# Layer 1 of a two-layer interaction kernel: the first two of its four groups go from whole fp32 matmuls to three high and low passes

## The chip, the cores and the metric

The kernel runs on one core of one Trainium2 chip. The metric is the time of one execution on the device in microseconds, the median of several runs. Engines are named as in the profile: PE is TensorE, DVE is VectorE, ACT is ScalarE, POOL is GpSimd, SP is SyncE.

## The reference

512 samples have 32 embeddings each of 32 numbers, gathered from 32 tables. Two interaction layers follow; then the sums over the last axis, joined with 16 dense numbers, go through three small dense layers.

```python
e = stack([tbl_f[ids[:, f]] for f in range(32)], axis=1)      # 512 x 32 x 32
x0, prev = e, e
for W in (filter_0, filter_1):                                # 1024 x 128 and 4096 x 128
    z = einsum('bhd,bmd->bhmd', x0, prev)                     # all pairs of fields
    z = z.reshape(b, h * m, d)
    prev = relu(einsum('bpd,pn->bnd', z, W[0]))
    outs.append(prev)
z = sum(concatenate(outs, axis=1), axis=-1)                   # 512 x 256
h = relu(concatenate([z, dense_ctx]) @ W_top1 + b_top1)
h = relu(h @ W_top2 + b_top2)
y = h @ W_top3
```

All is float32.

## The kernel before, in words

The batch is cut into 32 chunks of 16 samples, 512 columns (sample and embedding position) each; a chunk has four tiles of 128 columns.

**Layer 1.** A chunk's input lies 128 partitions wide in `x_shift` (four groups of shifted fields) and `x_same`. DVE multiplies them in `products`: `which` 0 makes groups 0 and 1 of `z` (one instruction of 128x1024, L520), `which` 1 makes groups 2 and 3, and `which` 2 makes `z_last` (L524), the half shift that needs its own rows. PE adds the groups into one bank, `acc1`, in `layer1` (L742 and after). Groups 0 and 1 (`WHOLE` is 2) are one fp32 matmul each (L751; the profile records it as two). Groups 2 and 3 (`SPLIT` is 2), from chunk 3 on, are three matmuls each of the type fp32r (L756): high weights by high rows, low weights by high rows, high weights by low rows. The high rows, `z_hi`, are ACT's rounding copy of both groups (`round_pair`, L397); the low rows, `z_lo`, are DVE's subtraction z - z_hi, one 128x512 instruction for each group (`lower_pair`, L530). The last matmul (L760) takes `z_parts`, whose rounding is ACT's (`round_last`, L392) and whose low third is POOL's (`lower_last`, L274). ACT then makes two copies of relu(acc1) (`relu1`, L379 and L384), and DVE makes the low part of the first (`lower`, L539).

**Layer 2.** For each tile PE fills eight banks, three fp32r matmuls for each (L784 to L786). By the order `ADADADAD` four banks go to ACT (`t_act`, a ring of three) and four to DVE (`t_dve`, a ring of four). ACT multiplies each quarter of its banks by a weight per partition (`weigh_tile`, L420); DVE multiplies each quarter of its own and adds it to what ACT left in `prod` (`add_tile`, L573 and L577, 16 instructions a tile). The first of DVE's additions of a tile waits for ACT's first bank of that tile. POOL then folds `prod` to one block: a DMA that adds one half to the other (`halve`, L283), then two additions, 128x512 and 128x256 (L303), and a third into `side` (L309). `halve` of a tile waits for ACT and DVE to be done with that tile; POOL issues `halve` of tile i and right behind it folds tile i-1.

**Order.** No planner is used: each engine's program is written out. In a chunk c of the steady state:

- PE: layer 2 of tile 0; groups 0 and 1 of layer 1 of chunk c+1; layer 2 of tile 1; the rest of layer 1 of c+1; layer 2 of tiles 2 and 3.
- DVE: `transpose` (L506) of c+1; tile 0; `lower_pair` of c+1; tile 1; `products` 0 and 2 of c+2; tile 2; `lower` of c+1; `sum2` (L597, L600) of c-1; tile 3; `products` 1 of c+2; `pooling1` (L548) of c+1.
- ACT: tile 0; `round_pair` of c+1; tile 1; `relu1` of c+1; tile 2; `relu2` of c-1 (L404); `round_last` of c+2; tile 3.
- POOL: for each tile in turn, two gathers of chunk c+3 (L264, tiles 0 and 1 only), `halve` of this tile, the fold of the tile before; at the end of the chunk `lower_last` of c+2.
- SP: the transposing round trip of the embeddings through device memory and the loads of `x_same`, `x_shift` and `x_pair`.

Of the kernel before, what the change touches and what calls it, by code (L numbers as in the profile page):

```python
# [6 lines left out]
MAPS = 128  # L7
# [5 lines left out]
RUN = TILES * DIM  # L13
SHIFTS = 4
GROUPS = 4
SPLIT = 2
WHOLE = GROUPS - SPLIT
BANK = 512
X_REST = 3 + 1

# [21 lines left out]
LEAD = 3  # L42


def dlrm_tower(nc, table, ids, dense, w0a, w0b, w0c, w1, wt1, bt1, wt2, bt2, wt3, identity, spread, out):
# [5 lines left out]
    with ExitStack() as ctx:  # L51
# [3 lines left out]
        def sem(name):  # L55
            return ctx.enter_context(nc.semaphore(name))
# [9 lines left out]
        x_shift = [sb(f"x_shift{p}", [128, GROUPS, COLS]) for p in range(2)]  # L66
        x_pair = [sb(f"x_pair{p}", [3 * FIELDS, 2, COLS]) for p in range(2)]
        z = [sb(f"z{p}", [128, GROUPS, COLS]) for p in range(2)]
        z_hi = sb("z_hi", [128, SPLIT, COLS], f32r)
        z_lo = sb("z_lo", [128, SPLIT, COLS], f32r)  # L70
        z_last = [sb(f"z_last{p}", [3 * FIELDS, COLS]) for p in range(2)]
        z_parts = [sb(f"z_parts{p}", [3 * FIELDS, COLS], f32r) for p in range(2)]
        v = sb("v", [128, GROUPS, MAPS])
        v_hi = sb("v_hi", [128, SPLIT, MAPS], f32r)
        v_lo = sb("v_lo", [128, SPLIT, MAPS], f32r)
        v_last = sb("v_last", [3 * FIELDS, MAPS])
        v_parts = sb("v_parts", [3 * FIELDS, MAPS], f32r)
        cur1 = [sb(f"cur1_{p}", [128, COLS]) for p in range(2)]
# [12 lines left out]
        turned2 = sb("turned2", [128, TILES * MAPS])  # L91
        pool2 = sb("pool2", [128, MAPS // DIM, TILES, CHUNKS])
        pool1 = sb("pool1", [128, TILES, CHUNKS * QUARTERS])
        ctx_sb = sb("ctx_sb", [CTX, BATCH])
        wt1_ctx = sb("wt1_ctx", [CTX, TOP1])
        bt1_sb = sb("bt1_sb", [128, T1])
        bt2_sb = sb("bt2_sb", [128, T2])
        wt3_sb = sb("wt3_sb", [128, T2])
# [5 lines left out]
        wt2_raw = w_raw[:, 2 * TOP1:2 * TOP1 + T1 * TOP2].rearrange("p (k n) -> p k n", k=T1)  # L104
        spare = 2 * TOP1 + T1 * TOP2 + T2 * BATCH
        pick = w_raw[:, spare:spare + QUARTERS * PICK].rearrange("x (q n) -> x q n", q=QUARTERS)
        h2 = w_raw[:, 2 * TOP1 + T1 * TOP2:2 * TOP1 + T1 * TOP2 + T2 * BATCH].rearrange("n (f b) -> n f b", f=T2)

        pool1_hi, pool1_lo = (sb(f"pool1_{half}", [128, BATCH], f32r)[:, :] for half in ("hi", "lo"))
        h1 = z[0]  # L110

        h1_hi, h1_lo = (w[:, 0:T1 * BATCH].rearrange("n (f b) -> n f b", f=T1) for w in (w_hi, w_lo))
# [32 lines left out]
        weigh_ready = sem("weigh_ready")  # L145
        z_ready = sem("z_ready")
        z_rounded = sem("z_rounded")
        pair_rounded, z_lo_ready = sem("pair_rounded"), sem("z_lo_ready")

        z_parts_ready = sem("z_parts_ready")  # L150
# [49 lines left out]
        @block.sync  # L200
        def _(sp):
            sp.dma_start(raw_ids[:, :], ids).then_inc(ids_loaded, 16)
            sp.dma_start(spread_sb[:, :, :], spread).then_inc(spread_loaded, 16)

            def chunk(c, p):
                turn = before(c, p) + 1

                wait(sp, layer1_done, c - 1)

                sp.wait_ge(gathered[p], turn * (16 * TILES))  # L210
                rows = x_rows[p].rearrange("h (q c) -> q h c", q=QUARTERS)
                sp.dma_start(rows[:, 0:FIELDS], emb[p][:, :]).then_inc(rows_written[p], 16)
                sp.dma_start(rows[:, FIELDS:2 * FIELDS], emb[p][:, :]).then_inc(rows_written[p], 16)

                sp.wait_ge(rows_written[p], turn * (16 * 2))
                src = x_rows[p]
                first, stride = src.offset, COLS
                pair = bass.AP(src.tensor, first, [[stride, FIELDS], [FIELDS // 2 * stride, 2], [1, COLS]])
                if c == 0:

                    sp.dma_start(x_pair[p][0:FIELDS, :, :], pair).then_inc(pair_zero, 16)
                    return

                def shifted(first_group, groups):

                    return bass.AP(src.tensor, first + first_group * stride,
                                   [[stride, FIELDS], [GROUPS * stride, SHIFTS], [1, groups * COLS]])

                sp.dma_start(x_same[p][:, :],
                             bass.AP(src.tensor, first, [[stride, FIELDS], [0, SHIFTS], [1, COLS]])).then_inc(x_first[p], 16)  # L230
                sp.dma_start(x_shift[p][:, 0:WHOLE, :].rearrange("p g c -> p (g c)"),
                             shifted(0, WHOLE)).then_inc(x_first[p], 16)
                for copy in range(3):
                    sp.dma_start(x_pair[p][copy * FIELDS:(copy + 1) * FIELDS, :, :], pair).then_inc(x_rest[p], 16)
                sp.dma_start(x_shift[p][:, WHOLE:GROUPS, :].rearrange("p g c -> p (g c)"),
                             shifted(WHOLE, SPLIT)).then_inc(x_rest[p], 16)

            def top_loads():

                sp.wait_ge(wl_ready, W_PIECES)  # L240
                sp.dma_start(ctx_sb[:, :], dense).then_inc(top_loaded, 16)
                sp.dma_start(pick[:, :, :], identity).then_inc(top_loaded, 16)
                sp.dma_start(wt1_raw, wt1[0:256, :].rearrange("(k p) n -> p k n", p=128)).then_inc(top_loaded, 16)
                sp.dma_start(wt1_ctx[:, :], wt1[256:256 + CTX, :]).then_inc(top_loaded, 16)
                sp.dma_start(bt1_sb[:, :], bt1).then_inc(top_loaded, 16)
                sp.dma_start(wt2_raw, wt2.rearrange("(k p) n -> p k n", p=128)).then_inc(top_loaded, 16)
                sp.dma_start(bt2_sb[:, :], bt2).then_inc(top_loaded, 16)
                sp.dma_start(wt3_sb[:, :], wt3).then_inc(top_loaded, 16)

            over_chunks(chunk, 4, top_loads)  # L250

            sp.wait_ge(y_ready, 1)
            sp.dma_start(out, y_sb[:, :]).then_inc(out_written, 16)
            sp.wait_ge(out_written, 16)
# [101 lines left out]
        def _(act):  # L356
# [29 lines left out]
            def round_last(c, p):  # L386
# [4 lines left out]
                wait(act, layer1_done, c - 1)  # L391
                nc.scalar.activation(z_parts[p][:, :], z_last[p][:, :], ACT.Copy).then_inc(z_rounded, 1)  # L392

            def round_pair(c, p):
                act.wait_ge(z_ready, c * 3 + 3)
                act.wait_ge(layer1_done, c)
                nc.scalar.activation(z_hi[:, :, :], z[p][:, WHOLE:GROUPS, :], ACT.Copy).then_inc(pair_rounded, 1)  # L397

            def relu2(c, p):

# [35 lines left out]
            def chunk(c, p):  # L436
                for i in range(TILES):
                    weigh_tile(c, i, p)
                    if i == 0 and not ((c < 2 or c + 1 >= CHUNKS)):
                        round_pair(c + 1, 1 - p)  # L440
                    if i == 2 and c == CHUNKS - 1:
                        upper_top(len(top_pieces) - 1)
                    if i == 1 and c == 0:
                        round_last(1, 1)
                    if i == 0 and 0 <= c - (CHUNKS - TOP_PEEL) < len(top_pieces) - 1:
                        upper_top(c - (CHUNKS - TOP_PEEL))
                    if i == 2 and not (c == 0):
                        relu2(c - 1, 1 - p)
                    if i == (2 if c == 0 else 1) and not (c + 1 >= CHUNKS):
                        relu1(c + 1, 1 - p)  # L450
                    if i == 0 and c == 1:
                        round_last(2, 0)
                    if i == 2 and not ((c == 0 or c + 2 >= CHUNKS)):
                        round_last(c + 2, p)

            for k in range(W_EARLY):
# [37 lines left out]
        def _(dve):  # L494
# [13 lines left out]
            def products(c, p, which):  # L508
# [14 lines left out]
                else:  # L523
                    nc.vector.tensor_tensor(z_last[p][:, :], x_pair[p][:, 0, :], x_pair[p][:, 1, :],  # L524
                                            ALU.mult).then_inc(z_ready, 1)

            def lower_pair(c, p):
                dve.wait_ge(pair_rounded, c - 2)
                for k in range(SPLIT):
                    nc.vector.tensor_tensor(z_lo[:, k, :], z[p][:, WHOLE + k, :], z_hi[:, k, :].bitcast(fp32),  # L530
                                            ALU.subtract).then_inc(z_lo_ready, 1)

            def lower(c, p):
# [59 lines left out]
            def sum2(c, p):  # L593
# [12 lines left out]
            nc.vector.tensor_tensor(v[:, :, :], v[:, :, :], v_b[:, :, :], ALU.add).then_inc(v_ready, 1)  # L606

            dve.wait_ge(v_ready, 1)
            nc.vector.tensor_copy(v_hi[:, :, :], v[:, WHOLE:GROUPS, :]).then_inc(v_ready, 1)
            dve.wait_ge(v_ready, 2)  # L610
            nc.vector.tensor_tensor(v_lo[:, :, :], v[:, WHOLE:GROUPS, :], v_hi[:, :, :].bitcast(fp32),
                                    ALU.subtract).then_inc(v_ready, 1)

            nc.vector.tensor_copy(v_parts[:, :], v_last[:, :]).then_inc(v_ready, 1)
# [41 lines left out]
            def chunk(c, p):  # L656
# [60 lines left out]
        def _(pe):  # L717
# [21 lines left out]
            def layer1(c, p, groups):  # L739
# [2 lines left out]
                    pe.wait_ge(lo_ready, c)  # L742
                    pe.wait_ge(cur1_ready, c)
                for g in groups:
                    if g < WHOLE or g < GROUPS and c <= 2:

                        if g == 0:
                            pe.wait_ge(z_ready, c * 3 + 1)
                        elif g == WHOLE:
                            pe.wait_ge(z_ready, c * 3 + 3)  # L750
                        nc.tensor.matmul(acc1[:, :], v[:, g, :], z[p][:, g, :], start=g == 0, stop=False)  # L751
                    elif g < GROUPS:
                        k = g - WHOLE
                        pe.wait_ge(z_lo_ready, (c - 3) * SPLIT + k + 1)
                        for weights, rows in ((v_hi, z_hi), (v_lo, z_hi), (v_hi, z_lo)):
                            nc.tensor.matmul(acc1[:, :], weights[:, k, :], rows[:, k, :], start=False, stop=False)  # L756
                    else:

                        pe.wait_ge(z_parts_ready, c)
# [195 lines left out]
```

## Time and profile before

| what | value |
|---|---|
| time, median of 3 runs | 865.25 us (864.55 to 865.81) |
| profiled execution, its own time | 865.07 us |
| its span, first to last instruction | 863.3 us |
| PE, DVE, ACT, POOL busy | 854.4, 778.2, 680.4, 655.3 us |
| granted TensorE clock, mean | 0.992 |

Busy time is the time in which at least one instruction of the engine was recorded as running. An instruction is recorded from when the engine takes it up, so in a run of DVE or ACT instructions each begins some 0.08 us ahead of the end of the one before, and an instruction that stands still for something inside the engine looks like a long one, not like idle time.

### The profile page before, as it was taken

How to read it: one execution, taken by the hardware profiler on the slowest of the kernel's cores; microseconds unless marked ns; L12 is line 12 of the kernel's file. 1: busy time of each engine (PE TensorE's matmuls, PEld its weight loads, DVE VectorE, ACT ScalarE, POOL GpSimd, SP SyncE). 2: the span in 40 equal slices, each digit the busy share in tenths (PEclk: the TensorE clock that was granted, in tenths of full speed). 3: DMA queues.
4: the chain of work that ended last, by engine and by line, in shares of the span. 5: the costliest groups of instructions: out<-in, count | busy, mean ns of one | idle time of the engine just before them, and what ended most of it. 6: DMA issues, size and time to landing. Idle time of an engine off the chain costs nothing.

```text
span 863.3 us, 13937 instructions
## 1 busy us (share of the span) xinstructions
PE 854.4 (99%) x3583; PEld 672.2 (78%) x3583; DVE 778.2 (90%) x2392; ACT 680.4 (79%) x2231; POOL 655.3 (76%) x677
## 2 busy tenths in 40 slices
PE   8999999999999999999999999999999999999998
PEld 3777787777778777777877777787777778777866
DVE  4889999999999999999999999999999999999952
ACT  3778888888888888888888888888888888888832
POOL 5577788888887888778788877778878878866740
PEclk9999999999999999999999999999999999999988
DMA  5878866668677666777666687766668776664500
GB/s 168 200 201 197 199 133 139 158 161 185 163 170 151 135 157 162 182 165 181 146 131 153 162 182 167 178 151 131 150 158 185 168 178 137 139 145 93 99 6 0
DMA packets 54949, 130.86 MB, mean 152 GB/s; under 512 B 8020, under 2 KB 18996, under 8 KB 54869
## 3 DMA queue, kind: packets, MB, share of 16 engines
q0 software_dynamic: 22240, 68.17, 42.9%
q1 hardware_dynamic: 31090, 59.13, 22.4%
q10 hardware_dynamic: 1539, 2.67, 0.9%
q8 instruction: 28, 0.46, 0.2%
q14 instruction: 52, 0.43, 0.1%
HBM read 59.69 MB, written 4.20 MB: 74 GB/s over the span
## 4 chain that ended last, share of the span: by engine, by line
PE 96%; DMA 2%; DVE 1%; POOL 0%; ACT 0%; issue 0%; SPq 0%; ACTq 0%
PE t_act L784 13%; PE t_act L786 13%; PE t_act L785 13%; PE t_dve L784 13%; PE t_dve L786 13%; PE t_dve L785 13%; PE acc L751 7%; PE acc L756 5%; PE t_act L794 1%; PE acc L760 1%; DMA x_rows<-emb 1%; PE t_dve L805 1%; PE t_dve L841 1%; PE t_act L862 0%; PE t_dve L855 0%; DVE prod L577 0%
## 5 line engine op out<-in xcount | busy, mean ns | idle before, releaser
L420 ACT ACTIVATE prod<-t_act,weigh 128x128 f32<-128x128 f32 x2048 | 576.5, 373 | 101.5 <-PE t_act L786 96.6
L577 DVE SCALAR_TENSOR_TENSOR prod<-t_dve,weigh,prod 128x128 f32<-128x128 f32 x1792 | 481.5, 342 | 9.4 <-PE t_dve L786 7.4
L303 POOL TENSOR_TENSOR prod<-prod 128x512 f32<-128x512 f32 (+1 forms) x255 | 296.8, 1164 | 19.6 <-DMA prod<-prod 8.8
L784 PE MATMUL t_act<-w_hi,cur_hi 128*128 128x512 f32 x512 | 212.3, 415 | 0.0
L786 PE MATMUL t_act<-w_hi,cur_lo 128*128 128x512 f32 x512 | 199.7, 390 | 0.0
L785 PE MATMUL t_act<-w_lo,cur_hi 128*128 128x512 f32 x512 | 199.6, 390 | 0.0
L784 PE MATMUL t_dve<-w_hi,cur_hi 128*128 128x512 f32 x512 | 199.5, 390 | 0.0
L786 PE MATMUL t_dve<-w_hi,cur_lo 128*128 128x512 f32 x512 | 199.3, 389 | 0.0
L785 PE MATMUL t_dve<-w_lo,cur_hi 128*128 128x512 f32 x512 | 199.1, 389 | 0.0
L283 POOL DMA_DIRECT2D prod<-prod x126 | 118.9, 944 | 104.6 <-ACT prod L420 63.2
L264 POOL DMA_INDIRECT emb<-table_dram,all_ids x128 | 163.8, 1279 | 40.0 <-issue 30.0
L784 PEld LDWEIGHTS t_act<-w_hi,cur_hi 128*128 128x128 f32 x512 | 96.2, 188 | 26.6 <-issue 8.0
L785 PEld LDWEIGHTS t_act<-w_lo,cur_hi 128*128 128x128 f32 x512 | 96.3, 188 | 26.3 <-issue 7.4
L785 PEld LDWEIGHTS t_dve<-w_lo,cur_hi 128*128 128x128 f32 x512 | 96.1, 188 | 20.6
L786 PEld LDWEIGHTS t_act<-w_hi,cur_lo 128*128 128x128 f32 x512 | 96.1, 188 | 20.6
L784 PEld LDWEIGHTS t_dve<-w_hi,cur_hi 128*128 128x128 f32 x512 | 96.1, 188 | 20.4
L786 PEld LDWEIGHTS t_dve<-w_hi,cur_lo 128*128 128x128 f32 x512 | 96.1, 188 | 20.4
L573 DVE SCALAR_TENSOR_TENSOR prod<-t_dve,weigh,prod 128x128 f32<-128x128 f32 x256 | 76.5, 340 | 36.4 <-ACT prod L420 33.1
L520 DVE TENSOR_TENSOR z<-x_shift,x_same 128x1024 f32<-128x1024 f32 x62 | 75.8, 1222 | 0.0
L309 POOL TENSOR_TENSOR side<-prod 128x128 f32<-128x128 f32 x127 | 61.4, 484 | 10.0
L751 PE MATMUL acc<-z,v 128*128 128x512 f32 x132 | 61.9, 591 | 0.0
L379 ACT ACTIVATE cur_hi<-acc 128x512 fp32r<-128x512 f32 x32 | 19.2, 599 | 39.4 <-PE acc L760 35.7
(93 smaller groups left out, 572.9 us busy)
## 6 DMA issues: line engine op xcount, KB each, us to landing
prod<-prod POOLq DMA_DIRECT2D x126, 512.0 KB, 5.1
x_shift<-x_rows SPq DMA_DIRECT2D x62, 512.0 KB, 5.9
x_pair<-x_rows SPq DMA_DIRECT2D x94, 128.0 KB, 4.3
x_same<-x_rows SPq DMA_DIRECT2D x31, 256.0 KB, 3.3
x_rows<-emb SPq DMA_DIRECT2D x64, 64.0 KB
w_raw<-w_dram ACTq DMA_DIRECT2D x8, 256.0 KB, 4.1
emb<-table_dram,all_ids POOLq DMA_INDIRECT x128, 2.9
w_raw<-wt_dram SPq DMA_DIRECT2D x2, 512.0 KB, 9.9
```

The source lines that it names most:

```text
L264: nc.gpsimd.indirect_dma_start(emb[p][:, i * DIM:(i + 1) * DIM], None, table, bass.IndirectOffsetOnAxis(ap=all_ids[:, c * TILES + i:c * TI ...
L283: nc.gpsimd.dma_start(prod[i][:, dst, :].rearrange("x h n -> x (h n)"), prod[i][:, other, :].rearrange("x h n -> x (h n)"), accum_op=ALU.a ...
L303: nc.gpsimd.tensor_tensor(src[:, dst, :], src[:, dst, :], src[:, other, :], ALU.add).then_inc(folded, 1)
L309: nc.gpsimd.tensor_tensor(side[p][:, i, :], src[:, 0, :], src[:, 1, :], ALU.add).then_inc(side_ready, 1)
L420: last = nc.scalar.activation(prod[i][:, HEADS * a + j, :], t_act[n % ARING][:, j * MAPS:(j + 1) * MAPS], ACT.Copy, scale=weigh[p][:, i, h ...
L520: nc.vector.tensor_tensor(z[p][:, g, :], x_shift[p][:, g, :], x_same[p][:, None, :].to_broadcast([128, 2, COLS]), ALU.mult).then_inc(z_rea ...
L573: nc.vector.scalar_tensor_tensor(dst, src, w, dst, ALU.mult, ALU.add).then_inc(added, 1)
L577: nc.vector.scalar_tensor_tensor(dst, src, w, dst, ALU.mult, ALU.add).then_inc(added, 1)
L751: nc.tensor.matmul(acc1[:, :], v[:, g, :], z[p][:, g, :], start=g == 0, stop=False)
L784: nc.tensor.matmul(bank[:, :], cur_hi[p][:, cols], w_hi[:, w], start=True, stop=False)
L785: nc.tensor.matmul(bank[:, :], cur_hi[p][:, cols], w_lo[:, w], start=False, stop=False)
L786: nc.tensor.matmul(bank[:, :], cur_lo[p][:, cols], w_hi[:, w], start=False, stop=True).then_inc(done, 1)
```

## The change

`z_hi`, `z_lo`, `v_hi` and `v_lo` hold all four groups. From chunk 3 on groups 0 and 1 are also three fp32r matmuls each, in the order of before. ACT has a new `round_first`, a rounding copy of groups 0 and 1 of chunk c+2, ahead of tile 3 of chunk c, where `round_last` was; `round_last` moves behind tile 3. DVE has a new `lower_first`, two subtractions of 128x512 for groups 0 and 1 of chunk c+2, behind tile 3 of chunk c: after `products` 1 of c+2 and ahead of `pooling1` of c+1. Both run in chunks 1 to 29. A new semaphore, `layer1_half`, tells ACT that PE has read the first two groups of the chunk before. The operands of the dense input and two of the top stage's tiles move into memory that is free by then.

```diff
-SPLIT = 2
-WHOLE = GROUPS - SPLIT
+WHOLE = GROUPS // 2
...
+            def round_first(c, p):
+
+                act.wait_ge(z_ready, c * 3 + 1)
+                act.wait_ge(layer1_half, c - 1)
+                nc.scalar.activation(z_hi[:, 0:WHOLE, :], z[p][:, 0:WHOLE, :], ACT.Copy).then_inc(first_rounded, 1)
...
-                    if i == 2 and not ((c == 0 or c + 2 >= CHUNKS)):
+                    if i == 2 and 0 < c < CHUNKS - 2:
+                        round_first(c + 2, p)
+                    if i == 3 and 0 < c < CHUNKS - 2:
                         round_last(c + 2, p)
...
+            def lower_first(c, p):
+                dve.wait_ge(first_rounded, c - LEAD + 1)
+                for g in range(WHOLE):
+                    nc.vector.tensor_tensor(z_lo[:, g, :], z[p][:, g, :], z_hi[:, g, :].bitcast(fp32),
+                                            ALU.subtract).then_inc(first_lo_ready, 1)
...
-            nc.vector.tensor_copy(v_hi[:, :, :], v[:, WHOLE:GROUPS, :]).then_inc(v_ready, 1)
+            nc.vector.tensor_copy(v_hi[:, :, :], v[:, :, :]).then_inc(v_ready, 1)
             dve.wait_ge(v_ready, 2)
-            nc.vector.tensor_tensor(v_lo[:, :, :], v[:, WHOLE:GROUPS, :], v_hi[:, :, :].bitcast(fp32),
+            nc.vector.tensor_tensor(v_lo[:, :, :], v[:, :, :], v_hi[:, :, :].bitcast(fp32),
...
                 if more2:
                     products(c + 2, p, 1)
+                    if c > 0:
+                        lower_first(c + 2, p)
                 if more1:
                     pooling1(c + 1, 1 - p)
...
-                    if g < WHOLE or g < GROUPS and c <= 2:
+                    if g < GROUPS and c < LEAD:
...
-                        pe.wait_ge(z_lo_ready, (c - 3) * SPLIT + k + 1)
-                        for weights, rows in ((v_hi, z_hi), (v_lo, z_hi), (v_hi, z_lo)):
-                            nc.tensor.matmul(acc1[:, :], weights[:, k, :], rows[:, k, :], start=False, stop=False)
+                        if g < WHOLE:
+                            pe.wait_ge(first_lo_ready, (c - LEAD) * WHOLE + g + 1)
+                        else:
+                            pe.wait_ge(z_lo_ready, (c - LEAD) * WHOLE + g - WHOLE + 1)
+                        nc.tensor.matmul(acc1[:, :], v_hi[:, g, :], z_hi[:, g, :], start=g == 0, stop=False)
+                        nc.tensor.matmul(acc1[:, :], v_lo[:, g, :], z_hi[:, g, :], start=False, stop=False)
+                        last = nc.tensor.matmul(acc1[:, :], v_hi[:, g, :], z_lo[:, g, :], start=False, stop=False)
+                        if g == WHOLE - 1:
+                            last.then_inc(layer1_half, 1)
```

## Rows read from the trace of the kernel before

**Rows 1.** Part 1 of the page: busy us, share of the span, instructions.
```profile
PE 854.4 (99%) x3583; PEld 672.2 (78%) x3583; DVE 778.2 (90%) x2392; ACT 680.4 (79%) x2231; POOL 655.3 (76%) x677
```

**Rows 2.** Part 4 of the page: the chain that ended last, by engine.
```profile
PE 96%; DMA 2%; DVE 1%; POOL 0%; ACT 0%; issue 0%; SPq 0%; ACTq 0%
```

**Rows 3.** Busy time by stretch: PE, PEld, DVE, ACT, POOL, clock, DMA, GB/s.
```profile
400.00:450.00 50.00, 50.00 (x215) 39.95 (x214) 47.17 (x149) 41.38 (x138) 40.75 (x43) 1.00 0.70 160
```

**Rows 4.** Who waited for whom: us in total, times, longest.
```profile
POOL prod L283 <- ACT prod L420: 63.2, 28, 2.7
...
DVE z_last L630 <- DMA x_pair<-x_rows: 3.5, 1, 3.5
```

**Rows 5.** The chain in order of time, 406 to 435: start us, us, what.
```profile
407.31 1.72 PE acc L751 x4
...
414.51 1.36 PE acc L756 x6
```

**Rows 6.** Groups by form: line, operation, count, busy us and mean ns, idle before.
```profile
L397 ACT ACTIVATE z_hi<-z 128x1024 fp32r<-128x1024 f32 x29 | 31.1, 1073 | 0.0
```

**Rows 7.** DVE's timeline over one chunk: start us, us, line, what.
```profile
405.53 0.57 DVE L573 SCALAR_TENSOR_TENSOR prod<-t_dve,weigh,prod 128x128 f32<-128x128 f32 x2
...
409.63 1.29 DVE L530 TENSOR_TENSOR z_lo<-z,z_hi 128x512 fp32r<-128x512 f32 x2
411.06 0.61 DVE L573 SCALAR_TENSOR_TENSOR prod<-t_dve,weigh,prod 128x128 f32<-128x128 f32 x2
...
415.59 1.22 DVE L520 TENSOR_TENSOR z<-x_shift,x_same 128x1024 f32<-128x1024 f32 x1
416.73 0.68 DVE L524 TENSOR_TENSOR z_last<-x_pair 96x512 f32<-96x512 f32 x1
418.36 0.61 DVE L573 SCALAR_TENSOR_TENSOR prod<-t_dve,weigh,prod 128x128 f32<-128x128 f32 x2 [0.95 <-ACT prod L420]
...
422.65 0.68 DVE L539 TENSOR_TENSOR cur_lo<-cur,cur_hi 128x512 fp32r<-128x512 f32 x1
...
428.72 1.22 DVE L520 TENSOR_TENSOR z<-x_shift,x_same 128x1024 f32<-128x1024 f32 x1
...
430.68 0.57 DVE L573 SCALAR_TENSOR_TENSOR prod<-t_dve,weigh,prod 128x128 f32<-128x128 f32 x2
```

**Rows 8.** POOL's timeline behind tile 3 of that chunk.
```profile
429.36 0.86 POOL L283 DMA_DIRECT2D prod<-prod  x1 [2.48 <-ACT prod L420]
429.95 2.42 POOL L303 TENSOR_TENSOR prod<-prod 128x512 f32<-128x512 f32 x2
```

**Rows 9.** DVE's timeline, a product and its follower near 768.
```profile
767.55 1.28 DVE L520 TENSOR_TENSOR z<-x_shift,x_same 128x1024 f32<-128x1024 f32 x1
768.75 2.18 DVE L524 TENSOR_TENSOR z_last<-x_pair 96x512 f32<-96x512 f32 x1
```

**Rows 10.** POOL's timeline at the same place.
```profile
768.18 0.87 POOL L283 DMA_DIRECT2D prod<-prod  x1 [0.43 <-issue]
768.78 2.76 POOL L303 TENSOR_TENSOR prod<-prod 128x512 f32<-128x512 f32 x2
```

**Rows 11.** DVE's timeline near 787: a pair of low parts.
```profile
787.12 3.38 DVE L530 TENSOR_TENSOR z_lo<-z,z_hi 128x512 fp32r<-128x512 f32 x2
```

**Rows 12.** POOL's timeline at the same place.
```profile
787.75 0.86 POOL L283 DMA_DIRECT2D prod<-prod  x1
788.35 2.75 POOL L303 TENSOR_TENSOR prod<-prod 128x512 f32<-128x512 f32 x2
```

**Rows 13.** DVE's timeline near 642.
```profile
643.05 0.95 DVE L524 TENSOR_TENSOR z_last<-x_pair 96x512 f32<-96x512 f32 x1
```

**Rows 14.** POOL's timeline at the same place.
```profile
642.12 1.33 POOL L309 TENSOR_TENSOR side<-prod 128x128 f32<-128x128 f32 x1
```

**Rows 15.** DVE's timeline near 52, chunk 1.
```profile
52.80 0.68 DVE L524 TENSOR_TENSOR z_last<-x_pair 96x512 f32<-96x512 f32 x1
```

**Rows 16.** POOL's timeline at the same place.
```profile
52.30 3.15 POOL L303 TENSOR_TENSOR prod<-prod 128x512 f32<-128x512 f32 x2
```

More of the change, by code:

```diff
@@ L68, in dlrm_tower @@
         z = [sb(f"z{p}", [128, GROUPS, COLS]) for p in range(2)]
-        z_hi = sb("z_hi", [128, SPLIT, COLS], f32r)
-        z_lo = sb("z_lo", [128, SPLIT, COLS], f32r)
+        z_hi = sb("z_hi", [128, GROUPS, COLS], f32r)
+        z_lo = sb("z_lo", [128, GROUPS, COLS], f32r)
         z_last = [sb(f"z_last{p}", [3 * FIELDS, COLS]) for p in range(2)]
@@ L73, in dlrm_tower @@
         v = sb("v", [128, GROUPS, MAPS])
-        v_hi = sb("v_hi", [128, SPLIT, MAPS], f32r)
-        v_lo = sb("v_lo", [128, SPLIT, MAPS], f32r)
+        v_hi = sb("v_hi", [128, GROUPS, MAPS], f32r)
+        v_lo = sb("v_lo", [128, GROUPS, MAPS], f32r)
         v_last = sb("v_last", [3 * FIELDS, MAPS])
@@ L106, in dlrm_tower @@
         pick = w_raw[:, spare:spare + QUARTERS * PICK].rearrange("x (q n) -> x q n", q=QUARTERS)
+        room = 2 * TOP1 + T1 * TOP2
+        ctx_sb = w_raw[0:CTX, room:room + BATCH]
+        wt1_ctx = w_raw[0:CTX, room + BATCH:room + BATCH + TOP1]
         h2 = w_raw[:, 2 * TOP1 + T1 * TOP2:2 * TOP1 + T1 * TOP2 + T2 * BATCH].rearrange("n (f b) -> n f b", f=T2)
-        pool1_hi, pool1_lo = (sb(f"pool1_{half}", [128, BATCH], f32r)[:, :] for half in ("hi", "lo"))
+        pool1_hi, pool1_lo = z_hi[:, 0, :], z_lo[:, 0, :]
         h1 = z[0]
@@ L147, in dlrm_tower @@
         z_rounded = sem("z_rounded")
+        layer1_half, first_rounded, first_lo_ready = sem("layer1_half"), sem("first_rounded"), sem("first_lo_ready")
         pair_rounded, z_lo_ready = sem("pair_rounded"), sem("z_lo_ready")
@@ L235, in chunk @@
                 sp.dma_start(x_shift[p][:, WHOLE:GROUPS, :].rearrange("p g c -> p (g c)"),
[L236 removed]
+                             shifted(WHOLE, GROUPS - WHOLE)).then_inc(x_rest[p], 16)
             def top_loads():
@@ L396, in round_pair @@
                 act.wait_ge(layer1_done, c)
-                nc.scalar.activation(z_hi[:, :, :], z[p][:, WHOLE:GROUPS, :], ACT.Copy).then_inc(pair_rounded, 1)
+                nc.scalar.activation(z_hi[:, WHOLE:GROUPS, :], z[p][:, WHOLE:GROUPS, :], ACT.Copy).then_inc(pair_rounded, 1)
             def relu2(c, p):
@@ L525, in products @@
                                             ALU.mult).then_inc(z_ready, 1)
+            def lower_first(c, p):
[3 more added lines that the diff above has]
+                                            ALU.subtract).then_inc(first_lo_ready, 1)
             def lower_pair(c, p):
                 dve.wait_ge(pair_rounded, c - 2)
-                for k in range(SPLIT):
-                    nc.vector.tensor_tensor(z_lo[:, k, :], z[p][:, WHOLE + k, :], z_hi[:, k, :].bitcast(fp32),
+                for g in range(WHOLE, GROUPS):
+                    nc.vector.tensor_tensor(z_lo[:, g, :], z[p][:, g, :], z_hi[:, g, :].bitcast(fp32),
                                             ALU.subtract).then_inc(z_lo_ready, 1)
@@ L750, in layer1 @@
                             pe.wait_ge(z_ready, c * 3 + 3)
-                        nc.tensor.matmul(acc1[:, :], v[:, g, :], z[p][:, g, :], start=g == 0, stop=False)
+                        last = nc.tensor.matmul(acc1[:, :], v[:, g, :], z[p][:, g, :], start=g == 0, stop=False)
+                        if g == WHOLE - 1:
+                            last.then_inc(layer1_half, 1)
                     elif g < GROUPS:
-                        k = g - WHOLE
-                        pe.wait_ge(z_lo_ready, (c - 3) * SPLIT + k + 1)
-                        for weights, rows in ((v_hi, z_hi), (v_lo, z_hi), (v_hi, z_lo)):
-                            nc.tensor.matmul(acc1[:, :], weights[:, k, :], rows[:, k, :], start=False, stop=False)
+                        if g < WHOLE:
[5 more added lines that the diff above has]
+                        last = nc.tensor.matmul(acc1[:, :], v_hi[:, g, :], z_lo[:, g, :], start=False, stop=False)
+                        if g == WHOLE - 1:
+                            last.then_inc(layer1_half, 1)
                     else:
```

2 lines of the change are left out of this document (removed).

## The prediction, made before the result was known

> **What bounds the kernel now.** I read the page's busy times first, then the chain, the busy time by stretch, the waits and last DVE's and POOL's timelines of one chunk. PE is busy 99% of the span [rows 1] and makes 96% of the chain [rows 2]; in a stretch of 50 us in the middle it is busy all 50, at the full clock, and DVE is busy 47.17 of the same 50 [rows 3]. So PE sets the period, and DVE stands close behind. From one tile 0 to the next is 430.68 - 405.53 = 25.15 us [rows 7]; I use 25.14, since PE repeats at that.
>
> What DVE would need if it never waited is less than its busy time, because an instruction that follows another starts inside the other's last 0.08 us. From starts in rows 7: tile 0 takes 409.63 - 405.53 = 4.10; the two low parts 1.29 - 0.08 = 1.21; tile 1 stands at 415.59 - 411.06 = 4.53, but is the same 16 instructions as tile 0, so 4.10 is work; products 0 and 2 take 1.14 + 0.60 = 1.74; tile 2 stands at 422.65 - 418.36 = 4.29, again 4.10 of work; from there through tile 3 428.72 - 422.65 = 6.07; the last product, the pooling and the transpose 430.68 - 428.72 = 1.96. The sum is 23.28 us of a 25.14 us period: 1.86 us to spare.
>
> **The change, part by part.** *PE.* Two fp32 matmuls (four records) take 1.72 us, the six fp32r matmuls that do the same for groups 2 and 3 take 1.36 [rows 5]. The first two groups change from the one to the other in chunks 3 to 31, 29 times: 29 x 0.36 = 10.4 us less. PE's own period becomes 24.78 us, and were PE to stay the bound, the profiled execution's 865.07 would become 854.7.
>
> *ACT.* One more rounding copy of 128x1024, 1.07 us [rows 6]. ACT is busy 41.38 of 50 us [rows 3], 20.8 of a period; with 21.9 of 24.78 it stays under PE. The copy goes ahead of tile 3, where a shorter one (the last part's rounding) leaves, so ACT's first bank of tile 3 is some 0.4 us late; DVE starts tile 3 only after 6.0 us of own work and, with what follows, later than before, which hides it. Uncovered it would be at most 0.4 us a chunk; I take 0. The last part's rounding, now behind tile 3, is read by POOL after its fold and by PE a chunk later; POOL stands idle 2.48 us ahead of that fold [rows 8], so 0.
>
> *DVE without disturbance.* Two more subtractions, 1.21 us by the pair that is there [rows 7]. The need becomes 23.28 + 1.21 = 24.49 us, 0.29 under PE's new period. DVE enters tile 0 some 1.2 us later against PE, but four banks are in its ring, and a bank takes it 4.10 / 4 = 1.03 us, so PE isn't held. Its wait for the rounding is met long before. If this were all, the answer would be 854.7.
>
> *DVE against POOL.* The place of the pair is what I take to decide. The trace holds five DVE instructions of two operands in ordinary memory that met POOL's folds. Near 768 a product ends at 767.55 + 1.28 = 768.83, the next starts at 768.75 and takes 2.18 us instead of 0.68 [rows 7, 9]; POOL's fold had started at 768.78, behind a `halve` from 768.18 to 769.05 [rows 10]. Near 788 the same: two low parts take 3.38 us instead of 1.29 [rows 11], the `halve` stands at 787.75 and the fold at 788.35 [rows 12]. Near 642 POOL's L309 takes 1.33 us, held until the product ahead is over, then runs first and the next DVE instruction takes 0.95 us, ending 644.00 - 643.45 = 0.55 us behind it [rows 13, 14]. So one of the two waits for the other to finish, and POOL, once there, got in between two DVE instructions that stood back to back. Against it: at 52.80 the product's follower ran undisturbed in 0.68 us while a fold that had started at 52.30 stood [rows 15, 16].
>
> Now the new place. Tile 3's end triggers `halve`; it starts 429.36 - 428.72 = 0.64 us behind the product's start and the fold 1.23 us behind it, for 2.48 us of idleness ahead show that POOL is ready and waits for exactly this event [rows 4, 8]. The product ends at 1.22. Today what follows is the pooling, which reads one operand, and it isn't held. In the changed kernel the first subtraction starts at 1.13. Against the product's end the `halve` then stands at -0.58 and the fold at +0.01; at 768 they stood at -0.65 and -0.05 and DVE lost. Since tile 3's end triggers both, this repeats in every chunk, however late DVE is.
>
> The price, with the product's start as 0: the subtraction ends as at 768, 770.93 - 768.78 = 2.15 us behind the fold's start, at 1.23 + 2.15 = 3.38, instead of 1.81. The fold's second step has queued up meanwhile; at 768 the two steps ended at 771.54, 0.61 us behind DVE's instruction. If that step gets in ahead of the second subtraction, as L309 did at 642, the latter ends at 3.38 + 0.61 + 0.55 = 4.54, instead of 1.13 + 1.29 = 2.42. So 2.12 us more a chunk; the bounds are 0 (52.80) and 2.2 (both held for whole folds, 1.6 + 0.6). I take 2.12, since 768 is the nearest row. DVE's need becomes 24.49 + 2.12 = 26.61, and DVE is the bound: 1.83 us over PE's period.
>
> The second low pair, behind tile 0, comes while POOL gathers [rows 7]; in the new order POOL's next `halve` is triggered by tile 0's end, and its fold would start near the end of that pair: POOL waits, not DVE. `lower` behind tile 2 may meet L309's end: 0 to 0.3 us, taken as 0, kept in the range.
>
> *The Trainium skill on this.* "SBUF — State Buffer", section "SBUF: two separate sides", says that DVE and GpSimd share one pair of ports, that a DVE instruction with two such inputs and a GpSimd instruction exclude each other for their whole length, and that whoever starts first has it. By that rule the first subtraction, which starts ahead of the fold, isn't held, and only the second is; the sum would be the second rival's. The row at 768 says otherwise, and the measurement decides.
>
> *The rest.* The weights' two conversions double, 0.3 to 0.7 us on DVE at the start, ahead of idle time of 3.5 us in which DVE waits for a DMA [rows 4]: 0, at most +0.7. The moved buffers cost nothing that I can see: same instructions, same queues, 0.
>
> **The sum.** 865.07 - 10.4 + 29 x 1.83 = 907.7. DVE can fall behind before PE stands still, and it makes that up in the last two chunks, which have no products: between one bank (1.03) and four (4.1), I take 3. That gives 904.7, say 905 us. The profiled execution is 0.18 us under the median of the runs, which changes nothing.
>
> **The rivals.** *No collision that counts* (DVE keeps its pair together as at 52.80, and POOL waits): PE stays the bound, 24.49 against 24.78, and the time is 854.7, up to 859 if DVE needs 0.15 more a chunk than I add up. For it: the row at 52.80, and that most low parts take 1.29 for two. Against it: those meet gathers, not folds. It is the case of the other side.
>
> *Only one of the two is held.* If the first passes and the fold enters ahead of the second: the first ends at 1.81, the fold 1.60 - 0.13 later (770.38, which is 0.55 ahead of DVE's end at 768, less 768.78; L309 at 642 saves 0.13 by having waited), the second 0.55 behind that, at 3.83, 1.41 late: DVE's need is 25.90 and the time 854.7 + 29 x 1.12 - 3 = 884. If only the first is held: 3.38 + 0.61 = 3.99, 1.57 late, 854.7 + 29 x 1.28 - 3 = 889. For them: the rule above; whether POOL's second step wins rests on one meeting at 642.
>
> *DVE's lateness feeds back through ACT or POOL* (relu1 later, PE waits for a low part, which delays tile 2 on DVE): PE can then lose up to 0.5 us a chunk on top, 905 + 14 = 919. For it speaks that tile 2 waited 0.95 us for ACT [rows 7]; against it, that a DVE that is late finds ACT done.
>
> **How the numbers follow.** Both held, 0.52, own range 896 to 914 (29 x 0.3 us either way). One held, 0.20. No collision that counts, 0.20. Feedback, 0.05. Something between, near 865, 0.03. The range 880 to 914 leaves out the fast case and little else. What this kernel can tell from no change is 0.2%, 1.7 us: faster 0.20, within 0.02, slower 0.78.
>
> **What would show it.** In the changed kernel's trace: PE's six passes for groups 0 and 1 in 1.36 us; a chunk period of 26.6 us; the two new subtractions at 2.2 and 1.16 us in place of 0.68 each, each ending 0.55 us behind a POOL addition; POOL's second step at 1.08 us instead of 0.74; idle time of PE of 1.8 us a chunk, ended by DVE; DVE nearly without idle time. New subtractions of 0.68 us each and a period of 24.8 us would make the prediction wrong, and a wait of PE ended by ACT or POOL would put the loss elsewhere.

## The result, and the profile after

The changed kernel takes 872.78 us (median of 4, 872.23 to 875.11), before 865.53 (864.55 to 868.05, 4 runs): a ratio of 1.009, interval 1.0065 to 1.0116. A later run of both gave 874.39 and 865.76, 1.0102 (1.0073 to 1.0131). It is slower, as forecast, but by 7 to 9 us and not by 40. The profiled execution took 872.23 us, its span is 870.4.

The page of the changed kernel: part 1, then the chain by engine, which answer to [rows 1] and [rows 2].

```profile
PE 858.7 (99%) x3641; PEld 676.1 (78%) x3641; DVE 824.7 (95%) x2450; ACT 699.2 (80%) x2260; POOL 708.8 (81%) x677
...
PE 69%; DVE 23%; issue 4%; DMA 2%; ACT 1%; POOL 0%; SPq 0%; DVEq 0%; ACTq 0%
```

PE's share of the chain fell from 96% to 69%, and DVE has 23%. The busy time of 250 us in the middle (PE, PEld, DVE, ACT, POOL, clock, DMA, GB/s), before and then after:

```profile
400.00:650.00 250.00, 250.00 (x1066) 199.78 (x1065) 236.24 (x738) 206.89 (x686) 203.38 (x209) 1.00 0.71 160
```

```profile
400.00:650.00 250.00, 249.62 (x1070) 198.25 (x1069) 249.66 (x747) 210.39 (x685) 220.76 (x208) 1.00 0.72 160
```

DVE went from 236.24 us to 249.66: it hardly ever stops. PE's busy share still looks full, but a matmul that waits for a bank is recorded as a long one, so the share hides it: the weight loads take 198.25 us, where the same program of PE with nothing to hold DVE (e5 below) gets through 206.84 in these 250 us. PE's waits tell it better. The waits of the changed kernel (us, times, longest):

```profile
PEld t_dve L808 <- DVE prod L592: 22.2, 47, 1.3
```

The row says that a weight load of PE waited for DVE to empty a bank. No such row exists before. DVE's timeline over one chunk of the changed kernel (start us, us, line), which answers to [rows 7], and POOL's of the same stretch, which answers to [rows 8]:

```profile
408.45 1.22 DVE L529 TENSOR_TENSOR z<-x_shift,x_same 128x1024 f32<-128x1024 f32 x1
409.58 1.29 DVE L539 TENSOR_TENSOR z_lo<-z,z_hi 128x512 fp32r<-128x512 f32 x2
...
411.61 0.57 DVE L588 SCALAR_TENSOR_TENSOR prod<-t_dve,weigh,prod 128x128 f32<-128x128 f32 x2
...
421.05 1.22 DVE L529 TENSOR_TENSOR z<-x_shift,x_same 128x1024 f32<-128x1024 f32 x1
422.18 0.69 DVE L533 TENSOR_TENSOR z_last<-x_pair 96x512 f32<-96x512 f32 x1
422.78 0.60 DVE L588 SCALAR_TENSOR_TENSOR prod<-t_dve,weigh,prod 128x128 f32<-128x128 f32 x2
...
426.92 1.64 DVE L554 TENSOR_TENSOR cur_lo<-cur,cur_hi 128x512 fp32r<-128x512 f32 x1
```

```profile
409.08 0.87 POOL L284 DMA_DIRECT2D prod<-prod  x1 [1.20 <-DVE prod L592]
409.85 2.99 POOL L304 TENSOR_TENSOR prod<-prod 128x512 f32<-128x512 f32 x2
...
421.10 2.08 POOL L310 TENSOR_TENSOR side<-prod 128x128 f32<-128x128 f32 x1
...
425.64 1.02 POOL L284 DMA_DIRECT2D prod<-prod  x1
426.28 2.88 POOL L304 TENSOR_TENSOR prod<-prod 128x512 f32<-128x512 f32 x2
```

Three things are to be seen. The new pair (L539 at 409.58) takes 1.29 us: it isn't held, and POOL's fold pays, 2.99 us for two additions instead of 2.42. DVE has next to no idle time: tile 2 no longer waits 0.95 us for ACT. And the low part behind tile 2 (L554, L539 of before) takes 1.64 us instead of 0.68, because POOL's fold has been running since 426.28. This last one takes 1.5 us or more in 20 of the 32 chunks. The period is 25.5 us (L554 at 401.41 and at 426.92), DVE's own 24.49 and 0.96.

The two-operand forms of DVE in the chunks, with their means (the last number but one) in the changed kernel:

```profile
L529 DVE TENSOR_TENSOR z<-x_shift,x_same 128x1024 f32<-128x1024 f32 x62 | 77.0, 1242 | 0.0
L554 DVE TENSOR_TENSOR cur_lo<-cur,cur_hi 128x512 fp32r<-128x512 f32 x32 | 44.1, 1380 | 1.1 <-ACT cur L385 1.1
L539 DVE TENSOR_TENSOR z_lo<-z,z_hi 128x512 fp32r<-128x512 f32 x58 | 38.4, 703 | 0.0
L545 DVE TENSOR_TENSOR z_lo<-z,z_hi 128x512 fp32r<-128x512 f32 x58 | 37.3, 683 | 0.0
L533 DVE TENSOR_TENSOR z_last<-x_pair 96x512 f32<-96x512 f32 x31 | 23.2, 749 | 0.0
```

Alone they take 1215 and 683 ns (the medians in the trace before). What a mean has above that, times the count, I call held time: here (1380 - 683) x 32 = 22.3 us for the low part behind tile 2 and 27.2 us in all; in the kernel before it is 5.2 us in all. It is read from one profiled execution of each kernel, and the changed kernel's second one (e8) has 31.1 us, so a difference of some 4 us between two kernels tells nothing.

### The profile page after: what moved, and what is told of

Same layout as the page of the kernel before. It is cut to its first block, busy times and chain, and to the rows that moved or that the text cites. A ratio compares the mean times of both kernels' runs of the same rounds, so it can differ in the third digit from the quotient of the medians.

```text
span 870.4 us, 14169 instructions
## 1 busy us (share of the span) xinstructions
PE 858.7 (99%) x3641; PEld 676.1 (78%) x3641; DVE 824.7 (95%) x2450; ACT 699.2 (80%) x2260; POOL 708.8 (81%) x677
## 4 chain that ended last, share of the span: by engine, by line
PE 69%; DVE 23%; issue 4%; DMA 2%; ACT 1%; POOL 0%; SPq 0%; DVEq 0%; ACTq 0%
DVE prod L592 13%; PE t_dve L808 10%; PE t_act L808 9%; PE t_dve L809 9%; PE t_dve L810 9%; PE t_act L809 9%; PE t_act L810 9%; PE acc L776 2%; DVE prod L588 2%; PE acc L777 2%; PE acc L778 2%; DVE cur_lo L554 2%; DVE z_lo L539 2%; DVE z_lo L545 1%; PE t_act L818 1%
## 5 line engine op out<-in xcount | busy, mean ns | idle before, releaser
L592 DVE SCALAR_TENSOR_TENSOR prod<-t_dve,weigh,prod 128x128 f32<-128x128 f32 x1792 | 474.6, 340 | 1.2 <-PE t_dve L810 0.9
L304 POOL TENSOR_TENSOR prod<-prod 128x512 f32<-128x512 f32 (+1 forms) x255 | 323.3, 1268 | 23.4 <-DMA prod<-prod 12.4
L808 PE MATMUL t_dve<-w_hi,cur_hi 128*128 128x512 f32 x512 | 204.5, 399 | 2.6 <-DVE prod L592 1.7
L808 PE MATMUL t_act<-w_hi,cur_hi 128*128 128x512 f32 x512 | 200.8, 392 | 0.0
L265 POOL DMA_INDIRECT emb<-table_dram,all_ids x128 | 151.8, 1186 | 39.5 <-issue 22.6
L808 PEld LDWEIGHTS t_dve<-w_hi,cur_hi 128*128 128x128 f32 x512 | 96.0, 188 | 40.9 <-DVE prod L592 22.2
L808 PEld LDWEIGHTS t_act<-w_hi,cur_hi 128*128 128x128 f32 x512 | 96.2, 188 | 21.2 <-issue 1.0
L310 POOL TENSOR_TENSOR side<-prod 128x128 f32<-128x128 f32 x127 | 95.9, 755 | 10.0
L588 DVE SCALAR_TENSOR_TENSOR prod<-t_dve,weigh,prod 128x128 f32<-128x128 f32 x256 | 75.8, 337 | 7.6 <-ACT prod L427 7.6
L529 DVE TENSOR_TENSOR z<-x_shift,x_same 128x1024 f32<-128x1024 f32 x62 | 77.0, 1242 | 0.0
L776 PE MATMUL acc<-z_hi,v_hi 128*128 128x512 f32 x116 | 47.3, 408 | 0.7 <-DVE z_lo L539 0.7
```

The lines of the kernel that those rows point to most:

```text
L265: nc.gpsimd.indirect_dma_start(emb[p][:, i * DIM:(i + 1) * DIM], None, table, bass.IndirectOffsetOnAxis(ap=all_ids[:, c * TILES + i:c * TI ...
L304: nc.gpsimd.tensor_tensor(src[:, dst, :], src[:, dst, :], src[:, other, :], ALU.add).then_inc(folded, 1)
L310: nc.gpsimd.tensor_tensor(side[p][:, i, :], src[:, 0, :], src[:, 1, :], ALU.add).then_inc(side_ready, 1)
L529: nc.vector.tensor_tensor(z[p][:, g, :], x_shift[p][:, g, :], x_same[p][:, None, :].to_broadcast([128, 2, COLS]), ALU.mult).then_inc(z_rea ...
L588: nc.vector.scalar_tensor_tensor(dst, src, w, dst, ALU.mult, ALU.add).then_inc(added, 1)
L592: nc.vector.scalar_tensor_tensor(dst, src, w, dst, ALU.mult, ALU.add).then_inc(added, 1)
```

## The experiments

Three theories are set against each other after the result. Theory A: DVE sets the period, its own work plus what POOL's additions hold it; PE's gain is real and lies hidden behind it. Theory B: the new waits and copies on ACT and PE cost the time. Theory C: DVE's added work alone does, wherever POOL is.

### The two halves of the change

**e1**, PE's half alone:

```diff
-                    if c > 0:
-                        lower_first(c + 2, p)
...
-                            pe.wait_ge(first_lo_ready, (c - LEAD) * WHOLE + g + 1)
+                            pe.wait_ge(first_rounded, c - LEAD + 1)
...
-                        last = nc.tensor.matmul(acc1[:, :], v_hi[:, g, :], z_lo[:, g, :], start=False, stop=False)
+                        last = nc.tensor.matmul(acc1[:, :], v_hi[:, g, :], (z_hi if g < WHOLE else z_lo)[:, g, :],
+                                                start=False, stop=False)
```

> Only PE's part: three passes for groups 0 and 1, ACT's new copy stays, but DVE's new pair of subtractions is left out and the third pass reads the high rows once more (so the low rows of these two groups are left out of the result). Theory A (DVE sets the period of the changed kernel, 25.51 us, because its new pair uses up its slack and its low part behind tile 2 waits 0.96 us for a POOL addition): DVE then needs at most 23.28 + 0.96 = 24.2 us, PE's 24.78 sets the period, 854 to 857 us. Theory B (the new waits and copies on ACT and PE cost the time): 862 or more.

Measured: 855.01 us against 865.42, ratio 0.9891 (0.9839 to 0.9943). That is the 854.7 of the prediction's PE step. The low part behind tile 2 stands at a mean of 1311 ns here too (held time 33.8 us in all), though the new pair isn't there: PE's shorter period alone took DVE's slack. What is left of it nearly covers the held time: PE waits 2.8 us for DVE in front of L807, where the changed kernel's L808 waits 22.2. B falls: ACT's copy, its new order and `layer1_half` are all in this kernel. Only PE's wait for the new low rows isn't (it waits for ACT's copy in its place); e5 below has that too.

**e2**, DVE's and ACT's half alone:

```diff
-                    if g < GROUPS and c < LEAD:
+                    if g < WHOLE or g < GROUPS and c < LEAD:
```

> Only DVE's and ACT's part: groups 0 and 1 stay whole fp32 matmuls, but the new copy and the new pair are made all the same and not used. Theory A: DVE needs 24.49 + 0.96 = 25.45 us against PE's 25.14, so 870 to 875 us, as slow as the whole change. Theory B: DVE still fits, 865 to 867 us.

Measured: 874.06 us, 1.0093 (1.0058 to 1.0127), as expected by A. As slow as the whole change although PE does what it did before; held time 27.9 us. So the whole change is DVE's time, and PE's 10 us don't show in it at all.

### Taking the wait away where it stands

**e3**, one operand of the low part from the matmul bank:

```diff
-                    cur1[p][:, :].rearrange("m (q i d) -> m i q d", i=TILES, q=QUARTERS),
+                    acc1[:, :].rearrange("m (q i d) -> m i q d", i=TILES, q=QUARTERS),
```

> The changed kernel, but the low part behind tile 2 takes its first operand from the matmul bank acc1 and not from the relu copy, so it has one operand in ordinary memory instead of two (its relu is left out). Same place, same length alone. Theory A with POOL and DVE excluding each other only over two such operands: this instruction stands at 0.7 us instead of 1.64, DVE needs 24.5 us, PE's 24.78 sets the period, 855 to 859 us. If the 0.96 us are a wait for something else: 872 us as before. If the meeting only moves to another instruction: about 865.

Measured: 869.49 us, 1.0042 (1.0020 to 1.0063). DVE's forms in e3:

```profile
L529 DVE TENSOR_TENSOR z<-x_shift,x_same 128x1024 f32<-128x1024 f32 x62 | 80.0, 1290 | 0.0
L545 DVE TENSOR_TENSOR z_lo<-z,z_hi 128x512 fp32r<-128x512 f32 x58 | 47.7, 861 | 0.0
L539 DVE TENSOR_TENSOR z_lo<-z,z_hi 128x512 fp32r<-128x512 f32 x58 | 41.5, 756 | 0.0
L533 DVE TENSOR_TENSOR z_last<-x_pair 96x512 f32<-96x512 f32 x31 | 26.8, 865 | 0.4 <-DMA x_shift<-x_rows 0.4
...
L554 DVE TENSOR_TENSOR cur_lo<-acc,cur_hi 128x512 fp32r<-128x512 f32 x32 | 21.6, 676 | 1.1 <-ACT cur L385 1.1
```

The low part falls from 1380 to 676 ns in the same place: with one operand in ordinary memory it isn't held by POOL's fold. But all the others rise, the pair behind tile 0 from 683 to 861. Held time is 24.6 us instead of 27.2: it moved. The median is 3 to 5 us below the changed kernel's, but the profiled execution, which these rows show, took 872.27 us, the longest of the ten, so they don't say what the shorter ones saved. Where nothing is held, the period of this kernel is 24.54 us, which is DVE's own work as measured.

**e4**, the low part ahead of tile 2:

```diff
                     products(c + 2, p, 2)
-                add_tile(c, 2, p)
                 if more1:
                     lower(c + 1, 1 - p)
+                add_tile(c, 2, p)
                 sum2(c - 1, 1 - p)
```

> The changed kernel with the low part moved from behind tile 2 to ahead of it, where POOL gathers. Theory A: it no longer meets a fold, 0.7 us instead of 1.64, period 24.8, 855 to 860 us. If other instructions meet POOL instead, 865 to 872. Theory C (the price is DVE's added work alone, wherever POOL is): 870 or more.

Measured: 871.75 us, 1.0071 (1.0040 to 1.0101). The low part's mean falls to 800 ns, the products' rises from 1242 to 1366 and the new pair's from 703 to 809. Held time 25.9 us. The same again; the 855 to 860 us of theory A didn't come, here or in e3.

### Taking POOL's side away

**e5**, no 128x512 and 128x256 additions:

```diff
-FOLDS = {8: [(slice(0, 4), slice(4, 8)), (slice(0, 2), slice(2, 4))],
+FOLDS = {8: [],
...
-                pool.wait_ge(folded, done + len(steps))
+                wait(pool, folded, done + len(steps))
```

> The changed kernel with POOL's 128x512 and 128x256 additions left out (so the result lacks them); the DMA that adds the halves, the third addition, the gathers and all of DVE's work stay. e3 and e4 removed the wait of the low part behind tile 2 and other instructions took it over (0.9 us a chunk either way). Theory A, now: DVE loses some 0.9 us a chunk to POOL's additions wherever it puts its two-operand instructions. Without most of them DVE needs 24.5 to 24.7 us, PE's 24.78 sets the period: 854 to 858 us, and the subtractions stand at 0.68. Theory C (DVE's added work and waits for other reasons): 868 or more.

Measured: 852.08 us, 0.9851 (0.9818 to 0.9885), 2 us under the range that was expected. DVE's forms in e5, the three that were held most elsewhere:

```profile
L529 DVE TENSOR_TENSOR z<-x_shift,x_same 128x1024 f32<-128x1024 f32 x62 | 75.4, 1217 | 0.0
...
L554 DVE TENSOR_TENSOR cur_lo<-cur,cur_hi 128x512 fp32r<-128x512 f32 x32 | 21.8, 681 | 1.3 <-ACT cur L385 1.3
L533 DVE TENSOR_TENSOR z_last<-x_pair 96x512 f32<-96x512 f32 x31 | 21.1, 680 | 0.0
```

Held time is gone (0.2 us), all of DVE's added work is there, and the time is PE's: from chunk 3 on the low part behind tile 2 comes every 24.73 us. C falls. The rest of POOL's program, its gathers, DMAs and third additions, holds DVE for nothing.

### Less work, and other orders

**e6**, three groups in three passes, one new subtraction (ACT's copy, too, is of one group only):

```diff
-                for g in range(WHOLE):
+                for g in range(1, WHOLE):
...
-                    if g < GROUPS and c < LEAD:
+                    if g == 0 or g < GROUPS and c < LEAD:
```

> The changed kernel with group 0 back as a whole fp32 matmul: three groups in three passes, one new subtraction on DVE instead of two. PE's period is 25.14 - 0.18 = 24.96 us, DVE's need 23.28 + 0.61 + 0.9 = 24.8. Theory A: PE is the bound by a hair, 865.4 - 29 x 0.18 = 860 us (859 to 863), faster than both kernels. Theory B or C: 867 or more.

Measured: 863.83 us, 0.9984 (0.9963 to 1.0005), 12 runs of it. PE makes 96% of the chain and waits 1.9 us for DVE, so the order of the bounds is as expected; but of the 5 us some 2 came, outside the 859 to 863 that were expected, and the interval touches 1. Held time is 23.1 us. The period is PE's 24.96 us up to the middle of the kernel and then wanders between 24.3 and 26.3.

**e7**, five banks for ACT in tile 3:

```diff
-ORDER = [FULL if False else EVEN for tile in range(CHUNKS * TILES)]
+ORDER = [FULL if tile % TILES == 3 and TILES < tile < (CHUNKS - 1) * TILES else EVEN for tile in range(CHUNKS * TILES)]
```

> The changed kernel with the order ADAADADA in tile 3 of chunks 1 to 30: five banks for ACT, three for DVE. DVE's need falls by 1.03 us to 24.5, ACT's rises by 1.12 to 23.0, POOL has one more addition a chunk. Theory A: PE is the bound, 855 to 859 us. If POOL's longer folds cost DVE more than 0.3 us on top, or ACT's rings stop PE: 862 to 868. Theory B: no gain, 872.

Measured: 892.47 us, 1.0322 (1.0289 to 1.0356), the plainest miss of the expectations. DVE's forms in e7:

```profile
L529 DVE TENSOR_TENSOR z<-x_shift,x_same 128x1024 f32<-128x1024 f32 x62 | 92.0, 1483 | 0.0
L554 DVE TENSOR_TENSOR cur_lo<-cur,cur_hi 128x512 fp32r<-128x512 f32 x32 | 51.3, 1603 | 2.9 <-ACT cur L385 2.9
...
L533 DVE TENSOR_TENSOR z_last<-x_pair 96x512 f32<-96x512 f32 x31 | 33.9, 1095 | 0.5 <-DMA x_shift<-x_rows 0.4
```

DVE has 30 x 1.03 = 31 us less of its own work, and is held 71.4 us instead of 27.2. POOL has one addition more in each of these 30 chunks and a longer first one, 1.4 us more by the records of its additions; that this is what makes most of DVE's forms stand longer is likely, but wasn't tested by itself. Held time less the work saved makes 13 us of the 18 to 20 that the kernel is slower than the changed one; the rest isn't taken apart. The kernel got slower by giving the bounding engine less to do.

**e8** is the changed kernel once more, on the chip of e5 to e7.

> The changed kernel once more beside the others on the same chip: 872 to 874 us where before is 865.

Measured: 874.39 us, as said above; held time 31.1 us.

**e9** makes the new pair one chunk later, ahead of the pair behind tile 0, and **e10** is e9 with the early low part of e4:

```diff
                 if more1 and not (c == 1):
+                    lower_first(c + 1, 1 - p)
                     lower_pair(c + 1, 1 - p)
...
-                    if c > 0:
-                        lower_first(c + 2, p)
...
-                if more and not first:
-                    layer1(c + 1, 1 - p, range(0, 2))
...
-                    layer1(c + 1, 1 - p, range(0, 2) if first else range(2, GROUPS + 1))
+                    layer1(c + 1, 1 - p, range(0, 2 if first else GROUPS + 1))
```

> The changed kernel with the new pair of subtractions made one chunk later, right ahead of the pair behind tile 0, where POOL gathers; PE does all of layer 1 behind tile 1, since the rows come later. DVE's own work is unchanged, 24.49 us. Theory A (time = PE's 24.78 or DVE's own work plus what POOL's additions hold it, whichever is longer): the two fold additions behind tile 3 no longer wait for DVE, POOL is 0.6 us earlier, and if that takes the low part behind tile 2 out of the fold, held time falls from 0.9 to 0.3 or less: 855 to 860 us. If the held time only moves, 870 to 874. If layer 1 in one block starves DVE or ACT: idle time on DVE, over 874.

> The same, and the low part behind tile 2 moved ahead of tile 2 as in e4, so that five of DVE's eight two-operand instructions a chunk stand where POOL gathers. Theory A: held time under 0.4 us, 855 to 860 us. If DVE waits at the early low part for the relu: idle time in its place. If held time only moves: 870.

Measured: 880.61 us, 1.0162 (1.0138 to 1.0185), and 874.81 us, 1.0088 (1.0059 to 1.0117); held time 30.3 and 26.6 us. So both missed the 855 to 860 of theory A. The low part behind tile 2 still meets POOL's fold in e9, mean 1449 ns. DVE isn't idle (249.04 us of the 250 in the middle); it is POOL's gather that now stands beside four subtractions (a row of e9's POOL timeline, DVE's pairs last from 417.73 to 420.22):

```profile
418.35 2.74 POOL L265 DMA_INDIRECT emb<-table_dram,all_ids  x1 [0.30 <-issue]
```

A gather beside nothing takes 0.97 us. So the window in which "POOL gathers" grew by what DVE put into it, and the fold behind it came later: it starts 15.9 us behind tile 0's start and the low part stands at 16.5, both 1.2 us later than in the changed kernel. Moving DVE's work there moved the meeting along. e9 is 6 us slower than the changed kernel. Of the 5.9 us between the two profiled executions, 3.7 lie at the two ends, from the second low part to the third (24.14 us instead of 22.44) and from the last but one to the last (25.70 instead of 23.75), and 2.2 in all the chunks between. So it isn't held time of the steady chunks alone; why the ends are longer stays open.

**e11**, e6 with the early low part (both edits shown above):

> Three groups in three passes (e6) with the low part ahead of tile 2. DVE's own work 23.89 us, PE's period 24.96. Theory A: up to 1.07 us of held time cost nothing, 859 to 862 us; e6 had 0.92 held and 25.09 of period.

Measured: 864.71 us, 0.9987 (0.9966 to 1.0009), not the expected 859 to 862. No better than e6; held time 29.7 us.

## Why the prediction was wrong

The side was right, the size wrong: 905 forecast, 873 measured, outside the range of 880 to 914. That DVE, held by POOL's additions, becomes the bound was right too. But the collision that the forecast rested on didn't happen, and the one that did was put at nothing; with the first at 0 and the second left at 0, the prediction's own sum gives 854.7, faster than before. So the side came out right by luck. By its own steps:

- *PE, 10.4 us less.* Right, or a little low: e1 gives 855.0, and e5, which has nothing to hold DVE, 852.1. PE's period in e5 is 24.73 us, not 24.78.
- *ACT, 0.* Right, by e1.
- *DVE's own need, 24.49 us.* Right: the period of 25.5 us with 0.03 us of idle time and 0.96 us at L554 leaves 24.5, and chunks of e3 in which nothing is held take 24.54. That it lies only 0.2 to 0.3 us under PE's period decided the sign, since any held time beyond that counts in full.
- *DVE against POOL, 2.12 us a chunk at the new pair.* This is the step that failed. The geometry was right (in 19 of 29 chunks the fold is recorded 0.00 to 0.04 us behind the product's end, `halve` at -0.58 or -0.59), the outcome was not. 57 of the 58 new subtractions weren't held; POOL waited: the new pair's held time is 1.2 us in the whole kernel and not 2.12 in each chunk. I had taken the meetings at 768, 788 and 642 [rows 9 to 14] as telling who wins, and 52.80 [rows 15, 16] as the exception. They differ in something that I had in front of me: at 767.55 the product took 1.28 us and not 1.22, at 787.12 the first of the pair was itself held, behind POOL's L274, at 641.85 the product took 1.27; at 52.80 nothing had been held. These are the rows of before for it, with one more meeting that goes the other way:

```profile
51.67 1.21 DVE L520 TENSOR_TENSOR z<-x_shift,x_same 128x1024 f32<-128x1024 f32 x1
...
641.85 1.27 DVE L520 TENSOR_TENSOR z<-x_shift,x_same 128x1024 f32<-128x1024 f32 x1
...
666.99 1.22 DVE L520 TENSOR_TENSOR z<-x_shift,x_same 128x1024 f32<-128x1024 f32 x1
668.12 0.95 DVE L524 TENSOR_TENSOR z_last<-x_pair 96x512 f32<-96x512 f32 x1
...
786.45 1.29 POOL L274 TENSOR_TENSOR z_parts<-z_last,z_parts 32x512 fp32r<-32x512 f32 x1
```

At 666.99 the product wasn't held and its follower was, by POOL's L309. The prediction's "five" meetings left it out. So the trace before told the two cases apart in four of five meetings only; it is the trace after that makes a count of it, in the last section. It isn't the order of arrival either: at 421.10 POOL's addition had stood waiting for 1.16 us when the product ended, and it didn't get in. In the steady state the product behind tile 3 begins free, and the pair behind it isn't held.

- *The rule of the Trainium skill* ("SBUF — State Buffer", "SBUF: two separate sides": who starts first has the ports for the whole instruction) was set against the row at 768 and lost there. The trace after agrees with it: the first subtraction of the pair is never held, and POOL waits. That POOL, which has waited, then gets in ahead of the second one was the prediction's own addition, since the page doesn't say who is next; it isn't so in 28 of 29 chunks. The figure worked out with it was 884.
- *`lower` behind tile 2, 0 to 0.3 us, taken as 0.* This is the other step that failed, and where the time is: 0.96 us at 426.92 and about as much or more in 19 other chunks of 32, 22.3 of 27.2 us of held time. I had placed it with POOL's times from the new order but kept the end of L309 as the thing to meet. What changed is DVE: with its slack used up it no longer waits for PE and ACT between tile 0 and tile 2, so the low part comes 426.92 - 411.61 = 15.3 us behind tile 0's start instead of 422.65 - 405.53 = 17.1 [rows 7], while POOL's fold starts 14.7 us behind it. In the kernel before, that fold starts 14.1 us behind tile 0 and both its steps are over at 16.6:

```profile
419.62 2.55 POOL L303 TENSOR_TENSOR prod<-prod 128x512 f32<-128x512 f32 x2
```

So the 1.8 us that DVE spent waiting on the way there (0.95 of them in front of tile 2) kept the low part clear of the fold. e1 fits this: it has no new pair, only a shorter period of PE, and its low part is held as well.

- *The sum.* With 0 for the pair instead of 2.12 and 0.96 for `lower` instead of 0, the same working gives 865.07 - 10.4 + 29 x (25.45 - 24.78) - 3 = 871.1, against 872.23 in the profiled execution. That the two agree so well is in part chance: the low part isn't held 0.96 us in every chunk, but the held time of all forms, 27.2 us, comes to about 29 x 0.96. The forecast fails by these two terms.
- *No collision that counts* (0.20) missed as well: no collision at the pair, but one elsewhere.

What I learned only from e3, e4, e9 and e10: held time isn't a property of a place. Four kernels with all of DVE's work (e3 with one operand in another memory, the others in other orders) were held for 24.6 to 30.3 us, the changed kernel for 27.2 and 31.1; only taking POOL's additions away (e5) ended it. Why it stays near 27 us through such different orders isn't shown. That both engines run nearly without a pause, so that a wait saved in one place lets DVE arrive earlier at the next fold, is my reading and was not tested by itself.

## What to carry to other kernels

When a change fills up the second-busiest engine, don't stop at its own work against the bound: what it waited for before also kept its instructions clear of another engine's, and with the slack gone they meet at other places than in the trace of before. Before taking a rare meeting as the price of a regular one, compare what stood ahead of it, not only the distances in time. And take the cheaper test first: leaving out the partner's instructions (e5) showed in one run what moving one's own in four did not.

## What the runs showed of the hardware

- A DVE instruction with two operands in ordinary memory and a POOL addition don't run together; one waits for the other's end (a held 128x512 subtraction, which takes 0.68 us alone, ends 0.55 us behind the end of POOL's). With one operand in the matmul bank, as in e3, it isn't held (676 ns in the place of 1380). DVE's 128x128 multiply-adds, which have one operand there, run beside POOL's folds: their mean is 340 ns in the changed kernel and 343 in e5, which has no folds.
- Who waits, between two such DVE instructions back to back with a POOL addition waiting at the first one's end: if the first hadn't been held (by over 0.02 us), the second wasn't held either in 69 of 72 cases of the traces before and after; if it had been, the second was held in 9 of 9. Over the eleven kernels other than e3 and e5, it is 414 of 436 and 154 of 160. This is a count of what stood together, not an experiment; why it is so stays open. A POOL addition that doesn't get in waits through both: 2.08 us for one of 0.46 (421.10).
- POOL's gathers hold up no DVE instruction (e5 has them all and 0.2 us of held time), but take longer themselves beside DVE's instructions of two operands: 2.1 us in the kernel before beside a product and its follower (median of 26), 0.97 beside nothing, and in e9 2.73 to 2.77 beside four subtractions.
